# Feed-forward as one sequence of row blocks, gate and up in one product, requantisation through PSUM

## The reference

```
x = x + _L0_attn_ref(_layernorm(x, axis=-1), ...)
x = x + _L0_ffn_ref(_layernorm(x, axis=-1), ...)

amax = jnp.max(jnp.abs(xb), axis=-1)          # act_quant: per token, per 128 columns
scale = amax / FP8_MAX + 1e-12
xq = (xb / scale[:, :, None]).reshape(T, K)
...
xdq = xq * xs per block; wdq = wq * w_scale per 128 x 128 block; return xdq @ wdq.T
...
g = linear_dsv3(xf, w1, w1_scale)
u = linear_dsv3(xf, w3, w3_scale)
h = jax.nn.silu(g) * u
y = linear_dsv3(h, w2, w2_scale)
```

## Time and profile before

| | us |
|---|---|
| median of 3 runs (1918.16 to 1920.56) | 1919.47 |
| the profiled execution | 1918.38 |
| its span, first to last instruction | 1916.6 |
| TensorE busy | 1820.9 (95%) |
| VectorE busy | 1301.1 (68%) |
| GpSimd busy | 1006.9 (53%) |
| ScalarE busy | 918.7 (48%) |
| chain that ended last | PE 87%, DVE 8%, issue 2% |

### The profile page before, as it was taken

One profiled execution on the slowest core, in us unless ns is written; L12 is line 12 of the kernel. 1 busy time (PEld: TensorE's weight loads), 2 busy tenths in 40 slices (PEclk: granted clock), 3 DMA queues, 4 the chain that ended last, 5 costly groups with the idle time before them and its releaser, 6 DMA issues.

```text
span 1916.6 us, 37316 instructions
## 1 busy us (share of the span) xinstructions
PE 1820.9 (95%) x11192; PEld 1484.7 (77%) x11192; DVE 1301.1 (68%) x2149; ACT 918.7 (48%) x1660; POOL 1006.9 (53%) x802
## 2 busy tenths in 40 slices
PE   5799999999999999999999999999999977989898
PEld 4677787778777877787778777877887756878887
DVE  6588638863886388638863886388648857777776
ACT  3566536643664366436643664366436632212221
POOL 4266636663666366536653666366636665233220
PEclk9899999999999999999999999999999988999999
DMA  2211101110111011101110111011101110111101
GB/s 91 61 52 51 34 12 51 51 33 12 51 51 33 12 51 51 33 12 51 51 33 12 51 51 33 12 51 51 33 12 52 40 48 20 41 44 36 40 11 45
DMA packets 43639, 74.90 MB, mean 39 GB/s; under 512 B 10356, under 2 KB 11508, under 8 KB 43608
## 3 DMA queue, kind: packets, MB, share of 16 engines
q1 hardware_dynamic: 42600, 73.12, 12.1%
q10 hardware_dynamic: 1008, 1.38, 0.2%
HBM read 70.35 MB, written 4.06 MB: 39 GB/s over the span
## 4 chain that ended last, share of the span: by engine, by line
PE 87%; DVE 8%; issue 2%; POOL 1%; ACT 1%; DVEq 0%; POOLq 0%; ACTq 0%
PE proj L743 15%; PE proj L745 15%; PE proj L744 15%; PE y L875 6%; PE y L929 6%; PE y L931 5%; PE y L930 5%; PE y L865 3%; PE trb L842 3%; PE diff L851 3%; DVE gated L1234 2%; PE misc L851 1%; PE y L743 1%; PE y L744 1%; PE y L745 1%
## 5 line engine op out<-in xcount | busy, mean ns | idle before, releaser
L743 PE MATMUL proj<-xhi,w_hi 128*128 128x512 f32 x1088 | 465.9, 428 | 5.6 <-DVE v L1057 5.6
L745 PE MATMUL proj<-xhi,w_lo 128*128 128x512 f32 x1088 | 425.9, 391 | 0.0
L744 PE MATMUL proj<-xlo,w_hi 128*128 128x512 f32 x1088 | 425.6, 391 | 0.0
L392 POOL TENSOR_TENSOR w_lo<-w_raw,w_hi 128x512 fp32r<-128x512 f32 x144 | 184.2, 1298 | 227.9 <-ACT w_hi L522 227.9
L1057 DVE SCALAR_TENSOR_TENSOR v<-proj,par_sb,v 128x510 f32<-128x510 f32 (+2 forms) x384 | 281.9, 741 | 15.0 <-ACT v L544 11.7
L448 POOL TENSOR_TENSOR g_lo<-gated,g_hi 128x512 fp32r<-128x512 f32 x128 | 164.8, 1290 | 190.4 <-ACT g_hi L675 189.8
L743 PEld LDWEIGHTS proj<-xhi,w_hi 128*128 128x128 f32 x1088 | 205.0, 188 | 75.2 <-issue 7.9
L745 PEld LDWEIGHTS proj<-xhi,w_lo 128*128 128x128 f32 x1088 | 204.8, 188 | 46.4
L744 PEld LDWEIGHTS proj<-xlo,w_hi 128*128 128x128 f32 x1088 | 205.4, 189 | 38.6
L1152 DVE TENSOR_TENSOR M<-diff,cb 128x512 f32<-128x512 f32 x256 | 170.1, 686 | 81.4 <-ACT diff L630 81.4
L929 PE MATMUL y<-wo_hi,g_hi 128*128 128x512 f32 x512 | 204.3, 399 | 5.5 <-POOL g_lo L448 5.1
(11 more groups left out here) (179 smaller groups left out, 3718.1 us busy)
## 6 DMA issues: line engine op xcount, KB each, us to landing
w_raw<-in_win SPq DMA_DIRECT2D x144, 256.0 KB, 2.7
wo_raw<-in_wout SPq DMA_DIRECT2D x64, 256.0 KB, 2.6
M<-in_w SPq DMA_DIRECT2D x14, 512.0 KB, 3.3
cb<-in_w SPq DMA_DIRECT2D x7, 512.0 KB, 3.3
row_l<-rows_l SPq DMA_DIRECT2D x192, 6.0 KB
out<-resid SPq DMA_DIRECT2D x8, 256.0 KB, 2.0
rows_l<-gated SPq DMA_DIRECT2D x9, 128.0 KB, 2.5
resid<-in_x SPq DMA_DIRECT2D x4, 256.0 KB, 4.6
```

Source lines behind the costliest of these rows:

```text
L392: e.tensor_tensor(w_lo[:, slot, i, :], w_raw[:, i, :], w_hi[:, slot, i, :].bitcast(F32), ALU.subtract).then_inc(split.sem, 1)
L743: e.matmul(o, hi_l, hi_r, start=first, stop=False)
L744: e.matmul(o, hi_l, lo_r, start=False, stop=False)
L745: return e.matmul(o, lo_l, hi_r, start=False, stop=last)
```

## The change

It has five parts. (1) `over_chunks` and the engines' programs treat the 56 blocks as one sequence: down of a chunk's last block is issued behind the first gate_up of the next chunk; VectorE does hidden(t+1) ahead of h_lower(t); the first chunk stands outside the loop, and in it row blocks 6 and 7 of the second norm are turned and split between the first blocks' work. TensorE waits for one split row block at a time. (2) Gate and up weights lie side by side, so `gate_up` has 12 matmuls of 512 columns in place of 24 of 256. (3) In `hidden` and `second_norm` the activation and its block maxima stay in PSUM (h in the place of up, the norm in `trb` and `misc`), and `requantise` multiplies each 128 columns by reciprocal and scale in one instruction that reads PSUM and writes SBUF: two for h, four for the norm. `gate_up` now waits for `f_h` in place of `f_guf`. The second norm's transposes use only the two `diff` banks. (4) The epsilon of both norms is added on GpSimd ahead of its power. (5) The halving of `rg` is folded into the constants ahead of the power.

```diff
 def over_chunks(eng, chunk):
-    with eng.Fori(0, NFC // 2) as p:
-        chunk(2 * p, 0, True)
-        chunk(2 * p + 1, 1, True)
-    chunk(NFC - 1, 0, False)
+    chunk(0, 0, True, True)
+    with eng.Fori(0, (NFC - 3) // 2) as p:
+        chunk(2 * p + 1, 1, True, False)
+        chunk(2 * p + 2, 0, True, False)
+    chunk(NFC - 2, 1, True, False)
+    chunk(NFC - 1, 0, False, False)
...
+        f_pair = M[:, :, :].rearrange("p k (w f) -> p w k f", w=2)
+        f_raw = [f_pair[:, 0, :, :], f_pair[:, 1, :, :], cb[:, 0:2, :]]
...
+        up_hi = [w_hi[:, :, :, :].rearrange("p a b f -> p (a b) f"), wo_hi[:, 0:4, :]]
+        up_lo = [w_lo[:, :, :, :].rearrange("p a b f -> p (a b) f"), wo_lo[:, 0:4, :]]
+        down_hi = [wo_hi[:, 4:6, :], wo_hi[:, 6:8, :]]
+        down_lo = [wo_lo[:, 4:6, :], wo_lo[:, 6:8, :]]
...
+        nbank = [trb, misc]
...
-        rdone = Tally(sem("rms_done"), 0, 0, 2)
+        rdone = Tally(sem("rms_done"), 0, 0, 1)
...
+        def turned_to(n, t):
+            return diff[t % 2] if n is n2 else xbank[t % 4]
...
-            def roots(n, at, first, count):
+            def roots(n, nmv, at, first, count):
+                pool.wait_ge(s_mv, nmv)
+                cols = slice(first, first + count)
+                e.tensor_scalar(rstd[:, cols], mv[:, cols, 1:2].rearrange("p t a -> p (t a)"), EPS, None, ALU.add)\
+                    .then_inc(n["var"], 1)
...
-                    for t in range(TT - 3, TT):
-                        x_upper(n2, t)
+                    x_upper(n2, TT - 3)
...
-                act.wait_ge(f_guf, TT * c + t + 1)
+                act.wait_ge(f_h, TT * c + t + 1)
...
+                    if first and t in (1, 2):
+                        x_upper(n2, TT - 3 + t)
...
+                ring = 2 if n is n2 else 4
+                if t >= ring:
+                    pe.wait_ge(n["lower"], t - ring + 1)
...
-                if not nxt:
-                    for t in range(TT - 2, TT):
-                        turn_x(n2, t, hs[:, t % 2, 0:HID])
             over_tiles(pe, step, window)
-            pe.wait_ge(n2["lower"], TT)
...
-                pe.wait_ge(f_guf, TT * c + t + 1)
-                for w in range(2):
-                    for k in range(KD):
-                        mm = three(proj[t % 2][:, w * FC:(w + 1) * FC],
-                                   xhi[:, k, t * P:(t + 1) * P], xlo[:, k, t * P:(t + 1) * P],
-                                   f_hi[par_][w][:, k * FC:(k + 1) * FC], f_lo[par_][w][:, k * FC:(k + 1) * FC],
-                                   k == 0, k == KD - 1)
+                pe.wait_ge(f_h, TT * c + t + 1)
+                if first:
+                    pe.wait_ge(n2["lower"], t + 1)
+                for k in range(KD):
+                    mm = three(proj[t % 2][:, :],
+                               xhi[:, k, t * P:(t + 1) * P], xlo[:, k, t * P:(t + 1) * P],
+                               up_hi[par_][:, k, :], up_lo[par_][:, k, :], k == 0, k == KD - 1)
...
-            def chunk(c, par_, nxt):
-                def down(t):
-                    pe.wait_ge(f_lod, 3 * c + 3)
-                    pe.wait_ge(f_htl, TT * c + t + 3)
-                    pe.wait_ge(f_acc, TT * c + t + 1)
-                    for k in range(2):
-                        mm = three(ybank[t % 2][:, :], ht_hi[:, t % 2, k, :], ht_lo[:, t % 2, k, :],
-                                   f_hi[par_][2][:, k * HID:(k + 1) * HID], f_lo[par_][2][:, k * HID:(k + 1) * HID],
-                                   k == 0, k == 1)
-                    mm.then_inc(f_y, 1)
+            gate_up(0, 0, 0, True)
...
+            def chunk(c, par_, nxt, first):
                 for t in range(TT):
                     if t < TT - 1:
-                        gate_up(c, par_, t + 1)
+                        gate_up(c, par_, t + 1, first)
                     elif nxt:
-                        gate_up(c + 1, 1 - par_, 0)
+                        gate_up(c + 1, 1 - par_, 0, False)
                     if t:
-                        down(t - 1)
-                    pe.wait_ge(f_h, TT * c + t + 1)
+                        down(c, par_, t - 1)
+                    elif not first:
+                        down(c - 1, 1 - par_, TT - 1)
+                    if first and t in (1, 2):
+                        pe.wait_ge(f_htl, t + 2)
+                        turn_x(n2, TT - 3 + t, hs[:, (TT - 3 + t) % 2, 0:HID])
+                    pe.wait_ge(f_h, TT * c + t + 3)
                     pe.wait_ge(f_htl, TT * c + t + 1)
+                    if first and t < 4:
+                        pe.wait_ge(n2["lower"], t + 5)
                     for k in range(2):
                         mm = e.transpose(diff[t % 2][:, k * P:(k + 1) * P], fh[:, 2 + t % 2, k * P:(k + 1) * P], ident[:, :])
                     mm.then_inc(f_tr, 1)
-                down(TT - 1)
+                if not nxt:
+                    down(c, par_, TT - 1)
...
-                e.tensor_scalar(rg[:, :], misc[:, 0:TT], 1.0 / (4 * TPG * P), EPS, ALU.mult, ALU.add)\
+                e.tensor_scalar(rg[:, :], misc[:, 0:TT], 1.0 / (TPG * P), 4.0 * EPS, ALU.mult, ALU.add)\
...
-                e.tensor_scalar(rg[:, :], rg[:, :], 0.5, None, ALU.mult).then_inc(rdone.sem, 1)
-                dve.wait_ge(rdone.sem, rdone.window(g, 2))
...
-                        variances(n2, TT + t + 1, t, 1)
...
-                    second_norm(TT - 1)
-                    for t in range(TT - 3, TT):
-                        x_lower(n2, t)
+                    x_lower(n2, TT - 3)
...
+                link(normalise(nbank[t % 2][:, :], t))
+                reciprocals(t, nbank[t % 2][:, :], nbank[(t + 1) % 2][:, 0:KD], KD, link)
                 if t >= 2:
                     dve.wait_ge(n2["turned"], t - 1)
-                dst = hs[:, t % 2, 0:HID]
-                link(normalise(dst, t))
-                quantise(t, dst, KD, link).then_inc(n2["x"], 1)
-            def quantise(t, buf, blocks, link):
+                requantise(hs[:, t % 2, 0:HID], nbank[t % 2][:, :], t, KD).then_inc(n2["x"], 1)
+            def reciprocals(t, src, peak, blocks, link):
                 q = qs[:, t % 2, 0:blocks]
-                x3 = buf.rearrange("p (n f) -> p n f", n=blocks)
-                link(e.tensor_reduce(q, x3, AX, ALU.max, apply_absolute_value=True))
-                link(e.tensor_scalar(q, q, 1.0 / FP8_MAX, 1e-12, ALU.mult, ALU.add))
+                link(e.tensor_reduce(peak, src.rearrange("p (n f) -> p n f", n=blocks), AX, ALU.max,
+                                     apply_absolute_value=True))
+                link(e.tensor_scalar(q, peak, 1.0 / FP8_MAX, 1e-12, ALU.mult, ALU.add))
                 link(e.reciprocal(qr[:, t % 2, 0:blocks], q))
-                scale = q.unsqueeze(2).broadcast_to([P, blocks, QB])
-                over = qr[:, t % 2, 0:blocks].unsqueeze(2).broadcast_to([P, blocks, QB])
-                link(e.tensor_tensor(x3, x3, over, ALU.mult))
-                return e.tensor_tensor(x3, x3, scale, ALU.mult)
+            def requantise(dst, src, t, blocks):
+                for n in range(blocks):
+                    cols = slice(n * QB, (n + 1) * QB)
+                    ins = e.tensor_scalar(dst[:, cols], src[:, cols], qr[:, t % 2, n:n + 1], qs[:, t % 2, n:n + 1],
+                                          ALU.mult, ALU.mult)
+                return ins
...
-                g2, h = fh[:, t % 2, :], fh[:, 2 + t % 2, :]
+                g2, h = fh[:, t % 2, :], proj[t % 2][:, FC:2 * FC]
                 chain(e.scalar_tensor_tensor(g2, g2, 1.0, proj[t % 2][:, 0:FC], ALU.add, ALU.mult))
+                chain(e.scalar_tensor_tensor(h, g2, 0.5, h, ALU.mult, ALU.mult))
+                reciprocals(t, h, proj[t % 2][:, 0:2], 2, chain)
                 dve.wait_ge(f_tr, n + 1)
-                e.scalar_tensor_tensor(h, g2, 0.5, proj[t % 2][:, FC:2 * FC], ALU.mult, ALU.mult)\
-                    .then_inc(f_guf, 1)
-                dve.wait_ge(f_guf, n + 3)
-                quantise(t, h, 2, chain).then_inc(f_h, 1)
+                requantise(fh[:, 2 + t % 2, :], h, t, 2).then_inc(f_h, 1)
...
+                    if first and t in (1, 2):
+                        x_lower(n2, TT - 3 + t)
+                    h_lower(t)
+                    if first and t == 0:
+                        second_norm(TT - 1)
                     if t:
-                        add_y(t - 1)
-                add_y(TT - 1)
+                        add_y(c, t - 1)
+                    elif not first:
+                        add_y(c - 1, TT - 1)
+                if not nxt:
+                    add_y(c, TT - 1)
```

79 lines of the change are left out of this document (36 added, 43 removed).

## The result

The changed kernel takes 1861.82 us (median of 4 runs, 1859.9 to 1863.36) beside 1918.82 us for the kernel before on the same chip: ratio 0.9706, 95% interval 0.9692 to 0.9721. The forecast was 1863. The profiled execution took 1863.36 with a span of 1861.6, the slowest of its four.

What follows compares the result with a forecast made beforehand. TensorE was taken as the bound, waiting 0.57 us a block on VectorE's stretched or late work. Window -9.1, start +0.4, head -11.8, blocks -35.3, tail -0.6 sum to -56.4: 1863 us, range 1855 to 1871, chance 0.70.

Steps and rivals of the forecast that it cites:

- Gate and up, 2.82 us: Feed-forward blocks: twelve 512-column matmuls take 2.82 us in place of 2.95, bounds 2.74 to 2.95; a block becomes 4.36.
- The waits at chunk ends: Feed-forward chunk ends: down now lies behind 12 matmuls, so TensorE's seven waits for h's lower part, 6.5 us, go.
- hidden: VectorE's work on h: two 128-column multiplications take 0.50 us, PSUM outputs cost 0; 1.05 us a block to spare.
- the third rival: Feed-forward blocks: VectorE becomes the bound through its outputs in PSUM, 1942 us at 0.5 more per instruction; chance 0.03.
- The collision: VectorE's multiplications of h and norm, stretched beside GpSimd (0.42 us to 1.88), were taken as freed by the PSUM form.
- The second rival: Feed-forward and window: VectorE still waits for GpSimd, 0.4 us for each of 3 a chunk; 1879 to 1891, say 1885; chance 0.11.
- The last window: Mixer's last window: VectorE runs ahead, TensorE's products run without waits and end at 1602.8 in place of 1611.9, 9.1 less.
- VectorE's step in the window: Last window: VectorE's work per row block falls from 5.4 us to 5.0, against TensorE's 5.97.
- The head: Window's end to block 4's gate_up: 20.5 us in place of 32.3, so 11.8 less; bounds 15 and 32.3.
- The first rival: Feed-forward's start: ScalarE's queue is blocked at late weight blocks, TensorE's clock falls, nothing gained there: 1875; chance 0.12.
- The start: Kernel's start: GpSimd's added epsilon ahead of its first power, which VectorE waits for, costs +0.4 us.
- The tail: Block 55's gate_up to the span's end: 14.1 us in place of 14.75, 0.6 less.

Runs made afterwards that it cites:

- e1: Changed kernel with gate and up again as 24 matmuls of 256 columns in place of 12 of 512: 1868.68 us, ratio 0.9738.
- e3: Changed kernel with the old order on both engines: h's lower part ahead of hidden, a chunk's last down product right behind its transposes: 1871.16 us, ratio 0.9752.
- e12: Changed kernel with only VectorE's order put back, h's lower part ahead of the next hidden: 1861.34 us, ratio 0.9705.
- e2: Changed kernel with h and its maxima in SBUF again and two 256-column multiplications, new order kept: 1929.17 us, ratio 1.0048.
- e5: Kernel before, with GpSimd's dequantisation of the feed-forward weights cut to one column of each 128: 1897.31 us, ratio 0.9889.
- e6: Kernel before, with h and its maxima kept in PSUM and requantised from there, all else as it was: 1895.93 us, ratio 0.9881.
- e10: Changed kernel with the epsilon of both norms added on VectorE again: 1862.43 us, ratio 0.9707.
- e11: Changed kernel with GpSimd dequantising the third weight block inside the last window and TensorE turning the last h ahead of down(54): 1858.91 us, ratio 0.9691.
- e4: Changed kernel with all eight row blocks of the second norm turned and split ahead of the first feed-forward product: 1870.1 us, ratio 0.9747.
- e9: Changed kernel with h in SBUF, new order, and ScalarE rounding each weight block behind its part of h: 1871.03 us, ratio 0.9759.

## Why the prediction was right, step by step

- **Gate and up, 2.82 us.** Measured 2.83, and a block 4.333 against 4.36. Undone alone it costs 6.9 us (e1). The small gain beyond the forecast in the 51 blocks, 36.7 for 35.3, is this 0.027 a block: down takes 1.37 for 1.39, the transposes 0.13 for 0.14, and 4.35 had been rounded up.
- **The waits at chunk ends.** Right: 9.3 us with the old places, and VectorE's order has no part in them by itself (e3 against e12).
- **hidden.** Two 128-column multiplications take 0.73 us (0.40 each, 0.32 apart), not 0.50; it lay inside the bounds 0.34 to 0.85 and costs nothing, as TensorE waits for h nowhere in the 51 blocks. h written to PSUM costs 0.429 against 0.420, so the 1.05 us bound was far off and the value 0 right; the third rival had no ground.
- **The collision.** The mechanism was right, and e2, e5 and e6 show it by itself: taken out of before it gives 21 to 22 us, put back into after it costs 67. The reason I gave for "gone" was looser than the chip: I said that no *large* instruction was copied from SBUF to SBUF, while in e2 one of two columns waits 2.04 us. The changed kernel escapes because its maxima moved to PSUM too. The trace of before already showed it, in rows that I had not read: line 1230, of two or four columns, takes 0.17 us, but 0.51 on six of its 56 two-column rows, and up to 1.54 on four columns:

```profile
1615.09 1.54 DVE L1230 TENSOR_SCALAR qs<-qs 128x4 f32<-128x4 f32 x1
```

- **The second rival's price was wrong.** I gave the collision, had it stayed, 0.4 us for each of three a chunk and 1885 us. e2 shows 1929. Two instructions collide, not one, because the new order puts hidden beside GpSimd's pair; the delay of 3.3 us is so far past the 1.05 to spare that TensorE waits 2.5; and the clock falls behind each wait. It was the real case of the other side, slower than before, and I had given that place to VectorE's cost in PSUM. Its condition did not occur, so the forecast stood.
- **The last window.** 9.8 for 9.1: TensorE has no wait left in it. Of the 9.8 us, 5.5 are gaps; the rest is slower matmuls (granted clock 0.88 before, 0.93 after). In before's window nine rows of the norm's instructions were stretched, by 7.2 us together, and after none is. But no run undid the norm's way through PSUM, so how much of the window's gain is that, and how much the row blocks that now come later, is not shown. The epsilon on GpSimd (0.22 us, taken as 0.3) is free, as e10 shows.
- **VectorE's step in the window** was mis-sized: I had 5.0 us a row block, and one takes 5.5. Four multiplications of 128 columns cost 1.37 us, as much as two of 512 (0.69 each), so the 0.5 us that I took off for them is not saved. Against TensorE's 5.9 that leaves 0.4 us to spare, where I had 1.0; it was enough, and VectorE still waits for TensorE:

```profile
1598.34 0.75 DVE L1207 SCALAR_TENSOR_TENSOR resid<-y,rg,resid 128x512 f32<-128x512 f32 x1 [0.59 <-PE y L947]
```

- **The head.** 20.7 us for 20.5. TensorE idles 2.74 for the 2.3 I had; gate_up(2) then takes 4.22 us (1613.08 to 1617.30) at a lower clock, 1.4 more than a dense one, where I had put 0.5 for it. The path to h(0) that I gave, through ScalarE's third weight block, is not the only one: VectorE's own queue ends at the same time, and in e11, with that block out of ScalarE's way, the first tanh starts 3.4 us behind the window's end in place of 5.8 and the wait stays 2.7. That the number came out so near is in part luck. The first rival (clock lost, nothing gained) fell: granted clock 0.92. e4 shows 8.3 of the gain of 11.7 by itself.
- **The start.** I had +0.4. The first normalisation begins at 13.90 for 13.59, but at 1538.98 both kernels stand level. That place lies from 1.0 us earlier to 1.5 later in the experiments that share the code ahead of it, so a few tenths can't be read there.
- **The tail.** The term failed in the profiled execution, 15.83 for 14.1. e10, with the same order of instructions there, took 14.0 with granted clock 1.00; after's tail has 0.74. What failed is one execution's clock, not the sum, and the same is true of the +2.1 us ahead of the window. The sum's parts came out otherwise than I had them, though: the wait for the last h (0.88 us before) is gone, and the wait for the lower part of block 54 grew from 0.97 to 1.81, as on VectorE it now stands behind hidden(55). Against the forecast's terms the two are 1.7 us each; window, head and blocks give 2.0 back, and the span's difference is 55.0 for 56.4.

Undone one at a time: 6.9 (width), 9.3 (order), 8.3 (norm), and for h in PSUM 22 on the old kernel, make 46.8, with the window's 9.8 some 56.6, nearly the whole of the gain of 57.0. That this adds up is in part luck: it hangs on the kernel that h in PSUM was measured in. In the changed kernel it is worth 67, in the changed kernel with the old order 32, in the kernel before 22.

## What to carry to other kernels

Where a chain holds an instruction that stretches until another engine's instruction has ended, ask when the other engine begins relative to the chain, not how busy it is: here its phase moved the same kernel by 58 us. A reordering that is worth 9 us on a clean chain can cost 26 on one that collides, so take the collision away first (here by keeping the values in PSUM) and reorder after. Price a rival by the place of its waits in the new order, and add the clock that falls behind each.

## What the runs showed of the hardware that I had not expected

- A VectorE instruction of two columns, SBUF to SBUF, takes 0.17 us and up to 2.04 beside GpSimd; the size does not protect. In the longest rows it ends with GpSimd's instruction (1758.96 and 1758.94 in e2); one of 256 columns ends 0.28 us behind it.
- Not every instruction waits: in e9 the maxima from SBUF to SBUF ran at 1748.33 in 0.42 us under GpSimd's row of 1748.02 to 1749.92, in e2 the reciprocal of two columns at 1758.99 in 0.17. The Trainium skill, "SBUF — State Buffer", section "Who interferes with whom", names tensor_reduce as one that never contends on this chip; e9's row agrees, and by e2's row the reciprocal, which that section does not list, didn't wait either.
- The two-scalar multiplication from PSUM costs 0.40 us for 128 columns, nearly what 256 columns of a product take (0.42); in a row they stand 0.32 apart.
- The same matmuls took 1.97 us in one execution and 3.68 in another, with a granted clock of 0.88 and 0.62 over that stretch; e5 and e12, with the code of before and of after there, have the first window product at 1556.43 and 1554.17, the other way round. A profiled execution can hold 2 to 4 us that belong to no edit, and only the comparison of several shows it.
